# Two moves and seventeen fillers in an attention and experts kernel: output additions ahead of group selection, a third row on VectorE, transposes of the identity in three waits

## The chip, the cores and the metric

The kernel runs on one core of a Trainium2 chip. The metric is the device time of one execution in microseconds, lowest is best. The core has five engines with queues of their own: TensorE (PE, matrix products into the eight banks of PSUM), VectorE (DVE), ScalarE (ACT), GpSimd (POOL) and SyncE (SP, which issues the loads and stores). Each executes its own list of instructions in order; semaphores are the only order between them. An instruction that has to wait holds up everything behind it on its engine.

## The reference

One layer of a transformer, in float32, for 2 sequences of 512 tokens of width 512. The input is normalised, and attention and a mixture of experts both read the normalised tokens; their outputs are added to the input.

```python
xn = _layernorm(x, axis=-1)
x = x + _L0_attn_ref(xn, Wq, Wk, Wv, Wo) + _L0_ffn_ref(xn, router_w, ...)
```

Attention has 32 query heads and 8 key heads of width 128, rotary positions and a causal mask. The feed-forward part has a router over 16 experts in 4 groups, and a shared expert that all tokens pass:

```python
logits = xt @ router_w + router_b
scores = softmax(logits) + router_bias
g = scores.reshape(T, GROUPS, E // GROUPS)
_, gidx = top_k(g.max(axis=-1), LIM)          # the two best groups
masked = where(keep[:, :, None], g, -inf).reshape(T, E)
_, idx = top_k(masked, K)                     # the two best experts in them
...
z = silu(xt @ sw1 + sb1) * (xt @ sw2 + sb2) @ sw3 + sb3   # the shared expert
return (y + z).reshape(shape)
```

## The kernel before

Float32 products are made of three: each operand is split into a rounded high part (`_hi`) and the rest (`_lo`), and `product` issues lo times hi, hi times lo and hi times hi (L1990, L1991, L1992). The high parts are copies on ACT or POOL, the low parts subtractions on DVE or POOL.

The 1024 tokens are eight blocks of 128, four for each sequence (batch 0 and 1). All five lists are written out by hand, in the order in which they run; there is no scheduler. The program has three stages.

First, the normalisation. For each batch DVE takes the statistics of four blocks (`moments`, L1224; `variances`; `scales`), then the blocks are normalised into `xn`: two of them on DVE (L1247), two on ACT (`normalise_rows`, L809). PE transposes the four blocks of a batch into four banks, 16 transposes (`transpose_rows`, L2009); ACT copies each bank to `xT_hi` (`hi_x`, L816), DVE subtracts to `xT_lo` (`lo_x`, L1253). Before `hi_x(0)` ACT also makes the high parts of the first weights of the shared expert (`hi_shared`, L804), from which POOL makes the low parts (L554). Ahead of the first transposes PE runs 38 transposes of the identity (L2086, `WARM`).

Second, the shared expert and the router. PE runs `up_first`, `up(1)`, the router's products, `up(2)`, `up(3)`, then `down(0)` and `down(1)`. `down` makes the output product of one block after the other, six matmuls of 512 columns each, in four banks that are used twice: the product of block n waits until the addition of block n - 4 is done. The wait in the code is `wait_count(pe, down_added, n - 3)`. DVE adds a product to the output `y` (`add_down`, L1310), for which POOL must have added the output's bias to the block before (`add_bias`, L569, counted by `y_biased`). Between, DVE computes the router: softmax, the best groups (`top_groups`, L1340 to L1346), the two best experts (`first_largest`, L1330 to L1356). The low part of the last hidden block is `h_lo` (L1265), which `down(1)` needs at its start.

Third, attention, head after head, with the experts' tiles between. PE first projects keys, values and queries of batch 0 (L1990 to L1992 with `wkv`, L2129 to L2131 with `wq`), while DVE turns the queries by their position (`turn_q1`, `turn_q2`, L1422 to L1430). `first_head(0)` is written out for the first key head: `scores` (L2176), `ranks` (the places of the tokens in the experts' tiles, L2103 to L2109), `project_kv`, and so on. A loop over six key heads and a last head follow.

Of the kernel before, what the change touches and what calls it, by code (L numbers as in the profile page):

```python
# [15 lines left out]
P = 128  # L16
B, T, D = 2, 512, 512
TB = T // P
# [17 lines left out]
S_BANKS, MOE_BANK, PROJ_BANK, OUT_BANKS, PT_BANKS, OT_BANK = (0, 1), 2, 3, (4, 3), (5, 6), 7  # L36
# [14 lines left out]
def wait_count(eng, sem, value):  # L51

    if not isinstance(value, int) or value > 0:
        eng.wait_ge(sem, value)


def count(per_step, g, b, k):

    return (2 * per_step) * g + (per_step * b + k)
# [38 lines left out]
def no_head(g):  # L98

    return isinstance(g, int) and not 0 <= g < KV  # L100
# [7 lines left out]
def build(nc, x, wq, wkv, wo, shared, sb3, w12, w3, b12, b3, router_w, router_b, router_bias,  # L108
# [8 lines left out]
    with ExitStack() as ctx:  # L117
        def sb(name, shape, dt=F32, stack=ctx):
            return stack.enter_context(nc.sbuf_tensor(name, shape, dt))

        def sem(name):
            return ctx.enter_context(nc.semaphore(name))
# [5 lines left out]
        ident = sb("ident", [P, P])  # L128
# [7 lines left out]
        bank = [ctx.enter_context(nc.psum_tensor(f"bank{i}", [P, 512], F32)) for i in range(8)]  # L136
# [107 lines left out]
        scale_ready, xn_dve, xn_act = sem("scale_ready"), sem("xn_dve"), sem("xn_act")  # L244
# [36 lines left out]

        block = ctx.enter_context(nc.Block())

        @block.sync
        def _(sp):

# [238 lines left out]
        def _(pool):  # L525
# [35 lines left out]
            pool.wait_ge(out_bias_in, 16)  # L561

            def add_bias(n):
                b, k = n // TB, n % TB
                if k < 2:
                    pool.wait_ge(xn_dve, 2 * b + k + 1)
                else:
                    pool.wait_ge(xn_act, 2 * b + k - 1)
                nc.gpsimd.tensor_tensor(y[:, n, :], y[:, n, :], out_bias[:, :], ALU.add).then_inc(y_biased, 1)  # L569

            pool.wait_ge(xn_dve, 4)
            for n in range(NB):
                add_bias(n)
            for s in range(2):
# [220 lines left out]
        def _(act):  # L795
# [9 lines left out]

            def normalise_rows(b):
                act.wait_ge(scale_ready, b + 1)
                for n in (TB * b + 2, TB * b + 3):
                    nc.scalar.activation(xn[:, n, :], y[:, n, :], ACT.Identity, bias=lnt[:, 5, n:n + 1],  # L809
                                         scale=lnt[:, 2, n:n + 1]).then_inc(xn_act, 1)  # L810

# [399 lines left out]
        def _(dve):  # L1211
            done = [0]

            def link(ins):

                done[0] += 1
                ins.then_inc(chain, 1)
                dve.wait_ge(chain, done[0])
# [15 lines left out]
            def scales(b):  # L1234
                cols = slice(TB * b, TB * b + TB)
                var, std, inv, tmp, half, shift = (lnt[:, k, cols] for k in range(6))
                dve.wait_ge(std_ready, b + 1)
                link(nc.vector.reciprocal(inv, std))

                nc.vector.tensor_scalar(half, inv, -0.5, None, ALU.mult)  # L1240
                link(nc.vector.tensor_tensor(tmp, inv, inv, ALU.mult))
                link(nc.vector.tensor_tensor(tmp, tmp, var, ALU.mult))
                link(nc.vector.scalar_tensor_tensor(inv, tmp, -3.0, half, ALU.add, ALU.mult))
                nc.vector.scalar_tensor_tensor(shift, mv[:, cols, 0], -1.0, inv, ALU.mult, ALU.mult)\
                    .then_inc(scale_ready, 1)
                for n in (TB * b, TB * b + 1):
                    nc.vector.tensor_scalar(xn[:, n, :], y[:, n, :], mv[:, n, 0:1], lnt[:, 2, n:n + 1],  # L1247
                                            ALU.subtract, ALU.mult).then_inc(xn_dve, 1)

# [57 lines left out]
            def add_down(n):  # L1307
                dve.wait_ge(down_psum, n + 1)
                dve.wait_ge(y_biased, n + 1)
                nc.vector.tensor_tensor(y[:, n, :], y[:, n, :], bank[DOWN_BANKS[n % 4]][:, :], ALU.add)\  # L1310
                    .then_inc(down_added, 1)
# [22 lines left out]
                link(nc.vector.tensor_tensor(result, spare, over_experts(most), ALU.is_equal))  # L1334

            hidden(3)
            for n in range(2):
                add_down(n)
            in_groups = score.rearrange("p n (g e) -> p n g e", g=GROUPS)
            link(nc.vector.tensor_reduce(grp[:, 0], in_groups, AX_X, ALU.max))  # L1340
# [4 lines left out]
                                         grp[:, 1].unsqueeze(3).broadcast_to([P, NB, GROUPS, EG]), ALU.mult))  # L1345
            link(nc.vector.tensor_tensor(masked_groups, masked_groups,  # L1346
                                         grp[:, 2].unsqueeze(3).broadcast_to([P, NB, GROUPS, EG]), ALU.add))
            for n in range(2, TB):
                add_down(n)
            spare, one, two = (pick[:, k] for k in range(3))  # L1350
            first_largest(one, masked, spare)
            link(nc.vector.scalar_tensor_tensor(masked, one, -BIG, masked, ALU.mult, ALU.add))
# [633 lines left out]
        def _(pe):  # L1986
# [10 lines left out]

            def transpose_rows(b):
                for k in range(TB):
                    if k == 0:  # L2000
                        pe.wait_ge(xn_dve, 2 * b + 1)
                    elif k == 1:
                        pe.wait_ge(xn_dve, 2 * b + 2)
                    else:
                        pe.wait_ge(xn_act, 2 * b + (k - 1))
                    for c in range(HC):
                        if k == 0:
                            wait_count(pe, xT_ok, HC * b + c - 3)
                        last = nc.tensor.transpose(bank[TR_BANKS[c]][:, k * P:(k + 1) * P],  # L2009
                                                   xn[:, TB * b + k, c * P:(c + 1) * P], ident[:, :])  # L2010
                        if k == TB - 1:
                            last.then_inc(xT_psum, 1)
# [122 lines left out]
            def project_kv(g, b, i, k, at=None):  # L2135

                if no_head(g):
                    return
                if b == 0 and k == 0:
                    pe.wait_ge(w_split, 6 * g + KV_ORDER)  # L2140
                if at is None and k == 0:
                    pe.wait_ge(q_turned, count(4, g, b, i))
                n = TB * b + 2 * i + k
                cols = slice(n * P, (n + 1) * P)
                last = product(bank[PROJ_BANK if at is None else at][:, k * 2 * P:(k + 1) * 2 * P],
                               [(xT_hi[:, c, cols], xT_lo[:, c, cols],
                                 wkv_hi[:, c].rearrange("p k o -> p (k o)"),
                                 wkv_lo[:, c].rearrange("p k o -> p (k o)")) for c in range(HC)])
                if k == 1:
                    last.then_inc(kv_psum, 1)  # L2150
# [120 lines left out]
            def expert_down(k):  # L2271
# [4 lines left out]
                pe.wait_ge(hT_split, k + 1)  # L2276
                product(bank[MOE_BANK][:, :], [(hT_hi[:, :], hT_lo[:, :], w3_hi[:, :], w3_lo[:, :])]).then_inc(edown_psum, 1)

            def first_ranks(g):

                if isinstance(g, int) and g == 0:
                    ranks()

            def first_head(g):
                scores(g, 0, 0, 0)
                first_ranks(g)
                project_kv(g, 1, 0, 0)
                scores(g, 0, 0, 1)
                project_kv(g, 1, 0, 1)
                scores(g, 0, 1, 0)  # L2290
                scores(g, 0, 1, 1)
                project_q(g, 1, 0, 0)
                project_q(g, 1, 0, 1)
# [505 lines left out]
```

## Time and profile before

| | |
|---|---|
| median of 3 runs | 905.96 us (905.58 to 906.03) |
| the profiled execution in all | 905.59 us |
| its span in the trace | 903.8 us |
| PE, DVE, ACT, POOL busy | 888.5, 677.7, 431.2, 526.5 us |
| granted TensorE clock, mean | 1.00 |

Times in the trace count from the start of the span. Busy is the time in which at least one instruction of an engine was at work; matmuls overlap, so PE's consecutive starts and not their durations tell its pace.

### The profile page before, as it was taken

To read this page: it belongs to the slowest core of one execution; us is meant where nothing else is said; L and a number is where in the kernel's file an instruction comes from. 1 tells how busy PE (TensorE), PEld (TensorE's weight loads), DVE (VectorE), ACT (ScalarE), POOL (GpSimd) and SP (SyncE) were. 2 spreads that over 40 slices of the span, in tenths; PEclk is the share of its full clock that TensorE was granted. 3 is DMA by queue.
4 is the path that set the end of the run, shared out by engine and by line. 5 is a ranking of instruction groups with operands and counts; after the bars stand their busy time and mean duration, and the time that the engine had idled before them with its cause. 6 is when DMAs were issued, how large, how long until landed. Compare 5 with 4: busy or idle time off the path is not lost.

```text
span 903.8 us, 17478 instructions
## 1 busy us (share of the span) xinstructions
PE 888.5 (98%) x5066; PEld 762.2 (84%) x5066; DVE 677.7 (75%) x1614; ACT 431.2 (48%) x1083; POOL 526.5 (58%) x638
## 2 busy tenths in 40 slices
PE   8997999999999999999999999999999999999998
PEld 7786887888888888888888889888888888888886
DVE  6688876687767876768767786768776787676886
ACT  3504543554535644454554545445453564454543
POOL 5923786565654765538554575356565476543663
PEclk9999999999999999999999999999999999999999
DMA  9910223143223532335222443224322252230242
GB/s 329 319 47 15 92 94 123 42 131 121 88 76 86 172 95 79 90 99 168 87 87 76 114 163 87 75 81 126 123 87 75 89 172 94 80 92 22 84 150 94
DMA packets 52161, 97.73 MB, mean 108 GB/s; under 512 B 5920, under 2 KB 17824, under 8 KB 52128
## 3 DMA queue, kind: packets, MB, share of 16 engines
q1 hardware_dynamic: 49568, 88.94, 31.7%
q0 software_dynamic: 2560, 8.39, 2.8%
q8 instruction: 16, 0.26, 0.1%
q14 instruction: 17, 0.14, 0.1%
HBM read 74.76 MB, written 22.54 MB: 108 GB/s over the span
## 4 chain that ended last, share of the span: by engine, by line
PE 92%; DVE 5%; issue 1%; ACT 1%; DMA 0%; POOL 0%; SPq 0%; DVEq 0%
PE bank L1992 10%; PE bank L1990 10%; PE bank L1991 10%; PE bank L2190 7%; PE bank L2129 7%; PE bank L2131 6%; PE bank L2130 6%; PE bank L2226 6%; PE bank L2222 6%; PE bank L2223 6%; PE bank L2206 4%; PE bank L2203 4%; PE bank L2204 4%; PE bank L2251 1%; PE bank L2176 1%
## 5 line engine op out<-in xcount | busy, mean ns | idle before, releaser
L636 POOL TENSOR_SCALAR prob<-prob,rsum 128x128 f32<-128x128 f32 (+3 forms) x256 | 143.9, 582 | 89.8 <-DVE rsum L1480 89.1
L876 ACT ACTIVATE prob<-bank,nmax 128x128 f32<-128x128 f32 (+3 forms) x256 | 133.7, 528 | 113.9 <-DVE nmax L1474 111.3
L1474 DVE CUSTOM_DVE_ANT_0 bank<-bank,causal 128x128 f32<-128x128 f32 (+3 forms) x256 | 122.8, 501 | 35.5 <-PE bank L1992 33.7
L1502 DVE TENSOR_TENSOR pT_lo<-bank,pT_hi 128x512 fp32r<-128x512 f32 x160 | 109.1, 684 | 29.0 <-ACT pT_hi L896 28.6
L896 ACT ACTIVATE pT_hi<-bank 128x512 fp32r<-128x512 f32 x160 | 95.0, 596 | 67.1 <-PE bank L2190 53.4
L2222 PE MATMUL bank<-wo_lo,oT_hi 128*128 128x512 f32 x256 | 106.2, 415 | 0.0
L2129 PE MATMUL bank<-xT_hi,wq_lo 128*128 128x512 f32 x256 | 104.7, 409 | 1.5 <-DVE v_lo L1458 1.4
L619 POOL TENSOR_TENSOR w_lo<-w_raw,w_hi 128x1024 fp32r<-128x1024 f32 x31 | 74.3, 2398 | 52.7 <-ACT w_hi L931 52.7
L2131 PE MATMUL bank<-xT_hi,wq_hi 128*128 128x512 f32 x256 | 101.1, 395 | 0.0
L2226 PE MATMUL bank<-wo_hi,oT_lo 128*128 128x512 f32 x256 | 100.7, 393 | 0.0
L2130 PE MATMUL bank<-xT_lo,wq_hi 128*128 128x512 f32 x256 | 100.6, 393 | 0.0
L2223 PE MATMUL bank<-wo_hi,oT_hi 128*128 128x512 f32 x256 | 100.5, 392 | 0.0
L585 POOL TENSOR_TENSOR q_first<-rot 128x128 f32<-128x128 f32 x60 | 28.3, 472 | 115.3 <-DVE rot L1430 115.1
L2190 PE MATMUL bank<-ident,prob 128*128 128x128 f32 x640 | 94.1, 272 | 0.0
L2190 PEld LDWEIGHTS bank<-ident,prob 128*128 128x128 f32 x640 | 77.7, 140 | 13.5
L1990 PE MATMUL bank<-wkv_hi,xT_lo 128*128 128x256 f32 x256 | 74.7, 292 | 1.1 <-DVE prob L1430 0.8
L1992 PE MATMUL bank<-wkv_hi,xT_hi 128*128 128x256 f32 x256 | 72.3, 282 | 0.0
L1991 PE MATMUL bank<-wkv_lo,xT_hi 128*128 128x256 f32 x256 | 71.9, 281 | 0.0
L1990 PE MATMUL bank<-kT_hi,q_lo 128*128 128x256 f32 (+2 forms) x192 | 68.0, 354 | 3.1 <-ACT prob L876 2.9
L887 ACT ACTIVATE oT_hi<-bank 128x512 fp32r<-128x512 f32 x64 | 38.1, 595 | 65.9 <-PE bank L2206 65.2
L2203 PE MATMUL bank<-pT_hi,v_lo 128*128 128x512 f32 x160 | 65.5, 409 | 0.5 <-DVE oT_lo L1487 0.5
L1991 PE MATMUL bank<-kT_lo,q_hi 128*128 128x256 f32 (+2 forms) x192 | 64.7, 337 | 0.0
(219 smaller groups left out, 2326.5 us busy)
## 6 DMA issues: line engine op xcount, KB each, us to landing
w_raw<-w SPq DMA_DIRECT2D x31, 512.0 KB, 3.5
wq_raw<-wq SPq DMA_DIRECT2D x32, 256.0 KB, 4.1
wo_raw<-wo SPq DMA_DIRECT2D x32, 256.0 KB, 2.8
xg<-x_slots SPq DMA_DIRECT2D x31, 256.0 KB, 3.5
w_raw<-w SPq DMA_DIRECT2D x31, 256.0 KB, 2.8
eb<-b SPq DMA_DIRECT2D x31, 256.0 KB, 3.9
y_slots<-eb SPq DMA_DIRECT2D x31, 256.0 KB, 2.5
x_slots<-pairs SPq DMA_DIRECT2D x3, 2048.0 KB, 16.0
```

Of the source, the lines that this page charges most:

```text
L636: last = nc.gpsimd.tensor_scalar(row, row, rsum[:, stat(b, i, h)], 1.0, ALU.mult, ALU.mult)
L876: last = nc.scalar.activation(prob[n % 2][:, h, 0:P * (i + 1)], bank[S_BANKS[use % 2]][:, 256 * k:256 * k + P * (i + 1)], ACT.Exp, bias=nm ...
L1990: nc.tensor.matmul(dst, a_lo, c_hi, start=start and k == 0, stop=False)
L1991: nc.tensor.matmul(dst, a_hi, c_lo, start=False, stop=False)
L1992: last = nc.tensor.matmul(dst, a_hi, c_hi, start=False, stop=stop and k == len(terms) - 1)
L2129: nc.tensor.matmul(q, wq_lo[:, h, col], xT_hi[:, c, span], start=c == 0, stop=False)
L2130: nc.tensor.matmul(q, wq_hi[:, h, col], xT_lo[:, c, span], start=False, stop=False)
L2131: last = nc.tensor.matmul(q, wq_hi[:, h, col], xT_hi[:, c, span], start=False, stop=c == HC - 1)
L2190: last = nc.tensor.transpose(bank[PT_BANKS[n % 2]][:, h * P:(h + 1) * P], prob[nth(g, b, i) % 2][:, h, j * P:(j + 1) * P], ident[:, :])
L2222: nc.tensor.matmul(dst, oT_hi[:, k, h], wo_lo[:, h, :], start=h == 0, stop=False)
L2223: nc.tensor.matmul(dst, oT_hi[:, k, h], wo_hi[:, h, :], start=False, stop=False)
L2226: last = nc.tensor.matmul(dst, oT_lo[:, k, h], wo_hi[:, h, :], start=False, stop=h == G - 1)
```

## The change

Three parts. The first changes which engine normalises which block: in batch 0 DVE takes blocks 0, 1 and 2 and ACT block 3; batch 1 stays at two and two. PE and POOL wait for the blocks accordingly. The second moves the additions of blocks 2 and 3 on DVE ahead of the group selection. The third puts transposes of the identity, which read and give nothing that is used, at three places of the first key head on PE: six after `ranks`, four and seven around `scores(g, 0, 1, 0)`; they write bank 7, which is free there.

```diff
+        DVE_ROWS, ACT_ROWS = (0, 1, 2, 4, 5), (3, 6, 7)
+
+        def wait_row(engine, n):
+            if n in DVE_ROWS:
+                engine.wait_ge(xn_dve, DVE_ROWS.index(n) + 1)
+            else:
+                engine.wait_ge(xn_act, ACT_ROWS.index(n) + 1)
...
-            pool.wait_ge(xn_dve, 4)
+            pool.wait_ge(xn_dve, len(DVE_ROWS))
...
-                for n in (TB * b + 2, TB * b + 3):
+                for n in ACT_ROWS[b:2 * b + 1]:
...
-                for n in (TB * b, TB * b + 1):
+                for n in DVE_ROWS[3 * b:3 * b + 3]:
...
             hidden(3)
-            for n in range(2):
+            for n in range(TB):
                 add_down(n)
             in_groups = score.rearrange("p n (g e) -> p n g e", g=GROUPS)
...
-            for n in range(2, TB):
-                add_down(n)
             spare, one, two = (pick[:, k] for k in range(3))
...
+            def keep_busy(g, k):
+
+                if isinstance(g, int) and g == 0:
+                    for _ in range(k):
+                        nc.tensor.transpose(bank[OT_BANK][:, 0:P], ident[:, :], ident[:, :])
...
             def first_head(g):
                 scores(g, 0, 0, 0)
                 first_ranks(g)
+                keep_busy(g, 6)
                 project_kv(g, 1, 0, 0)
                 scores(g, 0, 0, 1)
                 project_kv(g, 1, 0, 1)
+                keep_busy(g, 4)
                 scores(g, 0, 1, 0)
+                keep_busy(g, 7)
                 scores(g, 0, 1, 1)
```

The lists of the built programs show it in place. On ACT, at the start, the list before reads (a row is the line, the operation, what it writes and reads, and what it waits for; `xn` is a normalised block, `ew_hi` a weight's high part):

```order
L800 ACTIVATE lnt<-lnt 128x4 [waits var_ready]
L809 ACTIVATE xn<-y,lnt 128x512 [waits scale_ready]
L809 ACTIVATE xn<-y,lnt 128x512
L804 ACTIVATE ew_hi<-eraw 128x512 [waits eraw_first_in0]
L804 ACTIVATE ew_hi<-eraw 128x512 [waits eraw_first_in1]
L816 ACTIVATE xT_hi<-bank 128x512 [waits xT_psum] x4
```

and that of the change:

```order
L804 ACTIVATE lnt<-lnt 128x4 [waits var_ready]
L813 ACTIVATE xn<-y,lnt 128x512 [waits scale_ready]
L808 ACTIVATE ew_hi<-eraw 128x512 [waits eraw_first_in0]
L808 ACTIVATE ew_hi<-eraw 128x512 [waits eraw_first_in1]
L820 ACTIVATE xT_hi<-bank 128x512 [waits xT_psum] x4
```

One block less stands ahead of the weights and of the transposed input; on DVE a third one stands ahead of the statistics of batch 1. On DVE, behind the last hidden block, the list before reads (`y<-y,bank` is an output addition, `grp` and `beat` belong to the group selection, `red` and `pick` to the two best experts):

```order
L1265 TENSOR_TENSOR h_lo<-hid,h_hi 128x512 [waits h_hi_ok,h_ok]
L1310 TENSOR_TENSOR y<-y,bank 128x512 [waits y_biased,down_psum] x2
L1340 TENSOR_REDUCE grp<-route 128x32
L1319 TENSOR_TENSOR beat<-grp 128x128 [waits chain]
L1320 TENSOR_TENSOR beat<-grp 128x128 [waits chain]
L1321 TENSOR_TENSOR beat<-beat,before 128x128 [waits chain]
L1323 TENSOR_TENSOR beat<-beat 128x128 [waits chain]
L1324 TENSOR_REDUCE grp<-beat 128x32 [waits chain]
L1325 TENSOR_SCALAR grp<-grp 128x32 [waits chain]
...
L1346 TENSOR_TENSOR route<-route,grp 128x128 [waits chain]
L1310 TENSOR_TENSOR y<-y,bank 128x512 [waits y_biased,down_psum,chain]
L1310 TENSOR_TENSOR y<-y,bank 128x512 [waits y_biased,down_psum]
```

and that of the change:

```order
L1269 TENSOR_TENSOR h_lo<-hid,h_hi 128x512 [waits h_hi_ok,h_ok]
L1314 TENSOR_TENSOR y<-y,bank 128x512 [waits y_biased,down_psum] x4
L1344 TENSOR_REDUCE grp<-route 128x32
L1323 TENSOR_TENSOR beat<-grp 128x128 [waits chain]
L1324 TENSOR_TENSOR beat<-grp 128x128 [waits chain]
...
L1350 TENSOR_TENSOR route<-route,grp 128x128 [waits chain]
L1334 TENSOR_REDUCE red<-route 128x8 [waits chain]
```

The third and fourth addition went from behind the ten steps of the group selection to ahead of them. On PE, in the first key head, the list of the change has (the `ident` rows are the new ones; everything else stands as before):

```order
L2106 MATMUL bank<-chosen,ones 128x16 x8
L2280 MATMUL bank<-ident 128x128 x6
L1992 MATMUL bank<-wkv_hi,xT_lo 128x256 [waits q_turned]
...
L1994 MATMUL bank<-wkv_hi,xT_hi 128x256
L2280 MATMUL bank<-ident 128x128 x4
L1992 MATMUL bank<-kT_hi,q_lo 128x256 [waits exps_ok,q_split]
...
L1994 MATMUL bank<-kT_hi,q_hi 128x256
L2280 MATMUL bank<-ident 128x128 x7
L1992 MATMUL bank<-kT_hi,q_lo 128x256 [waits exps_ok,q_split]
```

Each group of fillers stands directly ahead of an instruction that waits, and waits for nothing itself.

## Rows read from the trace of the kernel before

**Rows 1.** The page: the span, and busy time of PE.
```profile
span 903.8 us, 17478 instructions
...
PE 888.5 (98%) x5066; PEld 762.2 (84%) x5066; DVE 677.7 (75%) x1614; ACT 431.2 (48%) x1083; POOL 526.5 (58%) x638
```

**Rows 2.** Waits of PE, whole span: us in total, times, longest.
```profile
PE bank L1990 <- DVE y L1310: 1.0, 1, 1.0
...
PE bank L2041 <- ACT xT_hi L816: 0.6, 1, 0.6
```

**Rows 3.** Timeline of ACT, 0 to 40: start us, us, line, operation [idle before].
```profile
9.02 1.52 ACT L809 ACTIVATE xn<-y,lnt 128x512 f32<-128x512 f32 x2 [1.11 <-DVE lnt L1244]
10.44 1.14 ACT L804 ACTIVATE ew_hi<-eraw 128x512 fp32r<-128x512 f32 x2
11.49 2.03 ACT L816 ACTIVATE xT_hi<-bank 128x512 fp32r<-128x512 f32 x4
...
22.11 2.07 ACT L816 ACTIVATE xT_hi<-bank 128x512 fp32r<-128x512 f32 x4 [2.59 <-PE bank L2009]
```

**Rows 4.** Timeline of PE, 0 to 60, its start-up.
```profile
2.57 6.62 PE L2086 MATMUL bank<-ident 128*128 128x128 f32 x38 [2.57 <-POOL ident L533]
9.49 1.99 PE L2009 MATMUL bank<-ident,xn 128*128 128x128 f32 x16 [0.30 <-DVE xn L1247]
12.11 2.19 PE L2041 MATMUL bank<-xT_hi,ew_hi 128*128 128x512 f32 x8 [0.63 <-ACT xT_hi L816]
...
15.96 1.98 PE L2051 MATMUL bank<-xT_lo,ew_hi 128*128 128x512 f32 x8
...
20.49 1.91 PE L2009 MATMUL bank<-ident,xn 128*128 128x128 f32 x16
```

**Rows 5.** Timeline of DVE, 0 to 40.
```profile
8.90 1.00 DVE L1247 TENSOR_SCALAR xn<-y,mv,lnt 128x512 f32<-128x512 f32 x2
9.81 2.47 DVE L1224 BATCH_NORM_STATS2 stats<-y 128x6 f32<-128x512 f32 x4
...
12.73 1.03 DVE L1232 TENSOR_SCALAR lnt<-mv 128x4 f32<-128x4 f32 x1
```

**Rows 6.** Timeline of POOL, 0 to 60.
```profile
11.22 2.52 POOL L554 TENSOR_TENSOR ew_lo<-eraw,ew_hi 128x512 fp32r<-128x512 f32 x2 [7.49 <-ACT ew_hi L804]
```

**Rows 7.** Timeline of DVE, 40 to 105.
```profile
44.26 0.83 DVE L1265 TENSOR_TENSOR h_lo<-hid,h_hi 128x512 fp32r<-128x512 f32 x1 [0.77 <-ACT h_hi L827]
45.01 1.27 DVE L1310 TENSOR_TENSOR y<-y,bank 128x512 f32<-128x512 f32 x2
...
49.22 1.28 DVE L1310 TENSOR_TENSOR y<-y,bank 128x512 f32<-128x512 f32 x2
...
61.60 0.69 DVE L1422 TENSOR_TENSOR rot<-bank,qc 128x512 f32<-128x512 f32 x1 [1.09 <-PE bank L2131]
...
64.39 0.69 DVE L1422 TENSOR_TENSOR prob<-bank,qc 128x512 f32<-128x512 f32 x1 [0.70 <-PE bank L2131]
```

**Rows 8.** Timeline of PE, 0 to 60, the output products of batch 1.
```profile
46.02 0.39 PE L1990 MATMUL bank<-ew_hi,h_lo 128*128 128x512 f32 x1
...
48.57 0.40 PE L1992 MATMUL bank<-ew_hi,h_hi 128*128 128x512 f32 x1
49.96 0.50 PE L1990 MATMUL bank<-ew_hi,h_lo 128*128 128x512 f32 x1 [0.98 <-DVE y L1310]
```

**Rows 9.** Timeline of PE, 60 to 100, waits around the fillers' places.
```profile
72.96 0.39 PE L1990 MATMUL bank<-wkv_hi,xT_lo 128*128 128x256 f32 x1 [0.82 <-DVE prob L1430]
...
77.60 0.36 PE L1990 MATMUL bank<-kT_hi,q_lo 128*128 128x256 f32 x1 [0.62 <-ACT prob L876]
...
79.59 0.35 PE L1990 MATMUL bank<-kT_hi,q_lo 128*128 128x256 f32 x1 [1.04 <-ACT prob L876]
...
80.82 0.50 PE L2129 MATMUL bank<-xT_hi,wq_lo 128*128 128x512 f32 x1 [0.29 <-DVE v_lo L1458]
```

**Rows 10.** Windows: busy us and instructions by engine, granted clock (PEclk), DMA share, GB/s.
```profile
70.00:90.00 20.00, 15.44 (x109) 12.75 (x108) 16.96 (x56) 8.73 (x26) 7.62 (x12) 1.00 0.05 15
```

More of the change, by code:

```diff
@@ L563, in add_bias @@
             def add_bias(n):
[L564 to L568, printed above, removed]
+                wait_row(pool, n)
                 nc.gpsimd.tensor_tensor(y[:, n, :], y[:, n, :], out_bias[:, :], ALU.add).then_inc(y_biased, 1)
-            pool.wait_ge(xn_dve, 4)
+            pool.wait_ge(xn_dve, len(DVE_ROWS))
             for n in range(NB):
@@ L1999, in transpose_rows @@
                 for k in range(TB):
[L2000 to L2005, printed above, removed]
+                    wait_row(pe, TB * b + k)
                     for c in range(HC):
```

## The prediction, written before the changed kernel ran

> **What bounds the kernel now.** The page comes first: TensorE (PE) is busy for 888.5 of the span's 903.8 us [rows 1], so only what lets PE start its work earlier can shorten the run, and at most some 15 us are there to be had. The list of waits, for PE, says which: the two that this change can touch are 1.0 us, once, for the output addition on VectorE (DVE), and 0.6 us, once, for the rounded copy of the transposed input on ScalarE (ACT) [rows 2]. The timelines then place them: the ACT wait ends at 12.11 us, the DVE wait at 49.96 us [rows 4, 8]. The three places of the fillers are PE waits of 0.82, 0.62 and 1.04 us, ending at 72.96, 77.60 and 79.59 us [rows 9]. Last the stretch from 70 to 90 us as a whole: PE busy 15.44 of 20 us, granted clock 1.00, the 2.4 GHz level [rows 10]. Between 12 us and 48.8 us PE has no wait of its own, so an earlier start there is handed on whole; what hands it on after that is checked below.
>
> **Part one, the normalised rows.** Before, ACT does two rows of batch 0 and then two rounded copies of the first weights, and only then the first copy of the transposed input, at 11.49 us; it stands in a row without a gap: rows from 9.02, weights from 10.44, transposed input from 11.49 [rows 3]. A row costs ACT (10.44 - 9.02) / 2 = 0.71 us of its time. With one row less the weights run from 9.73 to about 10.87 (their 1.14 us), and ACT is free 0.6 us sooner than now. Then PE's transposes decide. They need row 2 from DVE: DVE's pitch is (9.81 - 8.90) / 2 = 0.46 us and the second row ends at 9.90, so the third ends at about 10.35 [rows 5]. PE's 16 transposes start 0.115 us apart ((1.99 - 0.27 for the last one) / 15) from 9.49, so those of row 2 start at about 10.41 [rows 4]: DVE is ready 0.06 us ahead. They keep their times. When could ACT begin then? Batch 1 shows it with a free ACT: transposes from 20.49, first copy at 22.11, so 1.62 us later [rows 3, 4]; add the 0.08 us by which batch 0's block is longer (1.99 against 1.91) and it is 9.49 + 1.70 = 11.19 us. That is 11.49 - 11.19 = 0.30 us sooner. PE's first real matmul follows the first copy after 0.62 us and after it the copies set the pace (four in 2.03 us), so the whole block moves: **-0.30 us**. Its bounds: 0.15 if the DVE row is late by as much as its own margin twice over and semaphores take the rest; 0.60 if PE's last transposes did not matter and ACT's freedom were all that counts.
>
> What this makes later: DVE's statistics of batch 1 start 0.46 us later, at 10.27. At 12.73 a tiny DVE operation took 1.03 us, up to 13.76; GpSimd's (POOL) two splits run until 13.74 [rows 5, 6]. DVE waited there for POOL, so most of the 0.46 us is swallowed, since POOL's splits now also start up to 0.7 us sooner. The low part that DVE then makes is needed by PE only from 15.96 us, two microseconds on. Cost 0.
>
> The Trainium skill (SBUF — State Buffer, "SBUF: two separate sides") says that one port pair is shared by VectorE and GpSimd as an exclusive lock, and whichever begins first blocks the other for its whole instruction. This trace agrees, by the 1.03 us at 12.73. The rule speaks against a third SBUF-to-SBUF row on DVE: if POOL's split got in first, the row would be held for a split's 1.26 us and part one would lose about 0.6 us rather than gain. The third row starts at 9.81, and POOL can't begin before ACT's first weight copy ends at about 10.35, so I give that little.
>
> **Part two, the output additions.** PE's last output product but one (token block 6 of 8) reuses the bank of block 2 and waits until three additions are done. The products of block 5 end with the one that starts at 48.57; the next would start one step (0.23) later, at 48.80. It starts at 49.96 and takes 0.50 us where the one before took 0.40 [rows 8]. So the wait costs 49.96 - 48.80 + 0.10 = 1.26 us. In DVE's order two additions run from 45.01 to 46.28, group selection follows, and the third addition starts only at 49.22 [rows 7]. Moved up, the third runs from 46.28 to 46.9 and the fourth to 47.5 (0.60 us each). Are their products there? A block is six matmuls of 0.23 us, 1.40 us, and block 4's begin at 46.02 [rows 8]; so block 3's are out at about 46.2 and block 2's 1.4 us earlier, against additions that start at 46.9 and 46.3. Both are. PE wants the third at 48.80 (48.50 with part one) and has it 1.6 us before. **-1.26 us**; the low bound is 1.0, the idle time alone. Group selection starts 1.2 us later, but the steps behind it (the two largest) start where they did, since the same additions stood in front of them: DVE's total is the same, and the expert choice isn't delayed.
>
> Next to be late is h_lo, DVE at 44.26 for 0.83 us [rows 7], which PE's block 4 product wants at 46.02 [rows 8]. It has 0.9 us, or 0.6 when PE comes 0.30 sooner and DVE doesn't.
>
> Does the gain get through to 70 us? DVE turns the query projections into rotated ones and waits for PE there: 1.09 us before 61.60, 0.70 us before 64.39 [rows 7]. PE brings both 1.56 us sooner. If DVE doesn't move at all it starts the first 1.05 us sooner, ends it 0.5 us late against PE, and the 0.70 us make that up: it is busy with it for 64.39 - 0.70 - 61.60 = 2.09 us, so until 60.51 + 0.04 + 2.09 = 62.64, against 64.39 - 1.56 = 62.83. From there the whole chain of DVE, POOL and ACT to 81 us hangs on PE and moves as one. Behind 110 us PE hardly waits, so nothing absorbs it.
>
> **Part three, the fillers.** Nothing in the trace has exactly their place. The nearest rows are the transposes of rows 4: 0.115 us a piece in a warm stream, 6.62 / 38 = 0.174 us for the same instruction in the kernel's first microseconds [rows 4]. Six, four and seven cost 0.69, 0.46 and 0.81 us by the first and 1.04, 0.70 and 1.22 by the second; the waits are 0.82, 0.62 and 1.04 [rows 9]. By the first value all seventeen lie inside waits. I take it, because PE comes to the fillers out of 60 us of nearly unbroken work, as the transposes at 9.49 come out of a stream, and not from rest as the first 38 do. By the second they overrun by 0.22, 0.08 and 0.18, 0.48 us together, and even that has cover: PE still waits 0.29 us for DVE at 80.82 [rows 9], and the work that DVE, POOL and ACT do meanwhile doesn't come from the delayed products at once. **0**, with bounds of -0.3 (three restarts, each 0.1 us quicker because PE isn't idle in front) and +0.5.
>
> The waits' length doesn't change by parts one and two, since their two ends move together. The granted clock is 1.00 in this stretch already, so there is no clock to win back [rows 10]. The Trainium skill (TensorE: Matmul & The Clock Gate, "HAM oscillation — how this bites in real kernels") says that long idle gaps of the array let its clock fall to half and advises against them; by it fillers would pay where that happens. In this trace it doesn't happen, so by row and rule the sum is the same; only if other executions did fall would the page give more.
>
> **The sum.** -0.30 - 1.26 + 0 = -1.56 us. The profiled execution took 905.59 us in all, so its like would take 904.03; the median of the three runs is 0.37 us above it, 905.96, and from there 904.40. I forecast 904.4 us, 0.17% less. A measurement of this kernel tells about 0.2%, 1.8 us, from no change, so the likeliest result lies just inside that.
>
> **The rivals.**
> The gain arrives as summed (chance 0.58): with the bounds 0.15 to 0.6, 1.0 to 1.26 and 0.3 us between executions, 903.8 to 905.0.
>
> More than that (0.18): the restarts come quicker (0.3 us), or DVE's locks fall more kindly and ACT is freed by the full 0.6: up to 2.2 us, 903.4 to 903.9. For it speaks that each restart begins with a longer matmul, 0.50 against 0.40 for a 512-column one [rows 8]; against it that those products aren't what the chain waits for. A mild form is that the clock did fall in unprofiled runs: they differ by only 0.45 us, so it could give no more than that, 904.0.
>
> Less (0.18): DVE comes later than now. Its small steps from 38 to 44 us work on SBUF alone while POOL splits weights without a break, as the one at 12.73 did [rows 5, 6], and POOL's and DVE's phases now shift against each other; one more split to wait for is 1.3 us. Then h_lo misses its 0.6 us of cover and PE waits 0.7 us at block 4: 905.1. Or only part two works: 904.7. That the additions moved don't shorten anything would need block 3's product to come late, over 1 us later than it does.
>
> Slower than before (0.06): the fillers aren't covered. If they stand in front of products that were ready, all seventeen at 0.174 us are 2.96 us, less 1.56 gained: 907.4. It turns to slower once more than 1.56 us of them lie bare, that is more than half. Against it: three measured waits of 2.48 us in sum.
>
> **How the numbers follow.** The range leaves out the top of the last rival and the far ends: 903.6 to 905.6, which holds the first case, most of the less case and half of the second. Faster by over 0.2% means below 904.15: the whole of the second case, 0.18, and a third of the first, 0.18 more, 0.36 together. Slower by over 0.2% is above 907.8, which only a bad form of the last case reaches, 0.03. The rest, 0.61, is within 0.2%.
>
> **What the profile afterwards would show.** Part one: ACT's first copy of the transposed input near 11.2 us and the first matmul behind it near 11.8. Part two: no PE wait for the addition, the block 6 products starting one 0.23 us step behind block 5's, the key and value projections near 51.3 instead of 52.86. Part three: fillers of six, four and seven ending before their waits do, each wait's end 1.56 us earlier than now, and remaining idle times of 0.1 to 0.3 us. I am wrong if a new wait stands at 45 to 46 us for h_lo, if DVE's first rotation doesn't start by 60.6, or if the products behind the fillers start less than 1.4 us earlier than before.

## The result and the profile after

| | before | with the change |
|---|---|---|
| median, same chip | 906.38 us (20 runs) | 904.89 us (20 runs, 903.99 to 905.8) |
| ratio, 95% interval | | 0.9982 [0.9976, 0.9988] |
| the profiled execution in all | 905.59 us | 905.0 us |
| its span | 903.8 us | 903.2 us |
| granted TensorE clock, mean | 1.000 | 0.999 |

The change saves 0.18%, 1.6 us by the ratio: real by its interval, and just inside the 0.2% that the prediction called "no change". 904.4 us was forecast; 904.89 us was measured. Of the 0.49 us between them 0.42 is the starting point: the forecast started from 905.96 us, the median of three runs, and the twenty runs of the kernel before beside the change have 906.38. Three single runs of 1254, 1785 and 5045 us (two of the kernel before, one of e8) are left out of the ratios, means and counts below.

The page of the changed kernel, beside [rows 1]:

```profile
span 903.2 us, 17512 instructions
...
PE 890.6 (99%) x5083; PEld 764.3 (85%) x5083; DVE 676.9 (75%) x1615; ACT 430.2 (48%) x1082; POOL 525.8 (58%) x638
```

PE has the seventeen fillers more, DVE a normalised block more and ACT one less. The timeline of ACT at the start, beside [rows 3]:

```profile
9.08 0.81 ACT L813 ACTIVATE xn<-y,lnt 128x512 f32<-128x512 f32 x1 [1.11 <-DVE lnt L1248]
9.80 1.14 ACT L808 ACTIVATE ew_hi<-eraw 128x512 fp32r<-128x512 f32 x2
11.28 2.07 ACT L820 ACTIVATE xT_hi<-bank 128x512 fp32r<-128x512 f32 x4 [0.34 <-PE bank L2006]
```

The row of transposed copies now has an idle time of 0.34 us, and its releaser is PE: ACT is free before the first bank is ready, and PE's transposes decide. The timeline of DVE, beside [rows 5, 7]:

```profile
8.96 1.46 DVE L1251 TENSOR_SCALAR xn<-y,mv,lnt 128x512 f32<-128x512 f32 x3
10.33 2.47 DVE L1228 BATCH_NORM_STATS2 stats<-y 128x6 f32<-128x512 f32 x4
...
13.25 0.47 DVE L1236 TENSOR_SCALAR lnt<-mv 128x4 f32<-128x4 f32 x1
...
43.60 0.81 DVE L1269 TENSOR_TENSOR h_lo<-hid,h_hi 128x512 fp32r<-128x512 f32 x1 [0.77 <-ACT h_hi L831]
44.34 2.47 DVE L1314 TENSOR_TENSOR y<-y,bank 128x512 f32<-128x512 f32 x4
```

Three blocks in 1.46 us; the tiny operation that took 1.03 us takes 0.47; four additions stand together. The timeline of PE, beside [rows 4, 8, 9]:

```profile
9.56 2.01 PE L2006 MATMUL bank<-ident,xn 128*128 128x128 f32 x16
11.93 2.21 PE L2038 MATMUL bank<-xT_hi,ew_hi 128*128 128x512 f32 x8 [0.36 <-ACT xT_hi L820]
...
48.41 0.40 PE L1994 MATMUL bank<-ew_hi,h_hi 128*128 128x512 f32 x1
48.66 0.40 PE L1992 MATMUL bank<-ew_hi,h_lo 128*128 128x512 f32 x1
...
51.44 0.28 PE L1992 MATMUL bank<-wkv_hi,xT_lo 128*128 128x256 f32 x1
...
70.51 0.86 PE L2280 MATMUL bank<-ident 128*128 128x128 f32 x6
71.47 0.39 PE L1992 MATMUL bank<-wkv_hi,xT_lo 128*128 128x256 f32 x1
...
75.32 0.60 PE L2280 MATMUL bank<-ident 128*128 128x128 f32 x4
76.11 0.35 PE L1992 MATMUL bank<-kT_hi,q_lo 128*128 128x256 f32 x1 [0.19 <-ACT prob L880]
...
76.89 0.93 PE L2280 MATMUL bank<-ident 128*128 128x128 f32 x7
78.10 0.36 PE L1992 MATMUL bank<-kT_hi,q_lo 128*128 128x256 f32 x1 [0.28 <-ACT prob L880]
```

Block 6's products follow block 5's after 0.25 us, with no idle time. The ends of the three waits stood at 72.96, 77.60 and 79.59 [rows 9] and stand at 71.47, 76.11 and 78.10: 1.49 us earlier each. So at 80 us 1.49 us are won, and yet the two profiled spans differ by 0.6 only. Matmul by matmul PE is still 1.57 us ahead at 210.74 and 0.63 us at 217.79: the rest was given back there, in rows that the change doesn't touch. SP's queue, ACT and PE of the changed kernel, 199 to 218 us:

```profile
199.62 0.33 SPq L364 DMA_DIRECT2D w_raw<-w  x1
206.86 1.07 ACT L935 ACTIVATE w_hi<-w_raw 128x1024 fp32r<-128x1024 f32 x1 [2.32 <-DMA w_raw<-w]
217.79 0.39 PE L1992 MATMUL bank<-wkv_hi,xT_lo 128*128 128x256 f32 x1 [0.78 <-DVE rot L1432]
```

An expert's 512 KB of weights were issued at 199.62 and landed just before 206.86. The same two in the kernel before, where PE has no wait behind them:

```profile
201.49 0.33 SPq L356 DMA_DIRECT2D w_raw<-w  x1
207.00 1.06 ACT L931 ACTIVATE w_hi<-w_raw 128x1024 fp32r<-128x1024 f32 x1 [0.81 <-DMA w_raw<-w]
```

There the load took 5.5 us (207.00 - 201.49), here 7.2. Whether that is cause or chance is what the last experiment is for.

### The profile page after: what moved, and what is told of

Read it like the earlier page. It is cut to its first block, busy times and chain, and to the rows that moved or that the text cites. A ratio compares the mean times of both kernels' runs of the same rounds, so it can differ in the third digit from the quotient of the medians.

```text
span 903.2 us, 17512 instructions
## 1 busy us (share of the span) xinstructions
PE 890.6 (99%) x5083; PEld 764.3 (85%) x5083; DVE 676.9 (75%) x1615; ACT 430.2 (48%) x1082; POOL 525.8 (58%) x638
## 4 chain that ended last, share of the span: by engine, by line
PE 90%; DVE 4%; issue 3%; POOL 2%; ACT 1%; DMA 0%; another core or an unknown queue 0%; SPq 0%; DVEq 0%; POOLq 0%
PE bank L1992 10%; PE bank L1994 10%; PE bank L1993 10%; PE bank L2187 7%; PE bank L2126 6%; PE bank L2128 6%; PE bank L2127 6%; PE bank L2219 6%; PE bank L2223 6%; PE bank L2220 6%; PE bank L2203 4%; PE bank L2200 4%; PE bank L2201 4%; PE bank L2173 1%; PE bank L2248 1%
## 5 line engine op out<-in xcount | busy, mean ns | idle before, releaser
L1994 PE MATMUL bank<-kT_hi,q_hi 128*128 128x256 f32 (+2 forms) x192 | 64.7, 337 | 0.0
```

Source lines behind the costliest of these rows:

```text
L1994: last = nc.tensor.matmul(dst, a_hi, c_hi, start=False, stop=stop and k == len(terms) - 1)
```

## The experiments

Time is given as the ratio to runs of the kernel before on the same chip, whose median was 904.34 us in the first group of four kernels, 904.47 in the second and 904.54 in the third. As these ratios carry about 0.9 us of uncertainty, small terms are read from the traces, between two fixed points of one execution. Three are used: DVE's first normalised block (D), PE's first real matmul (M), PE's first key projection (K).

| kernel | D | M | M - D | K | K - D |
|---|---|---|---|---|---|
| before | 8.90 | 12.11 | 3.21 | 52.86 | 43.96 |
| before again | 8.72 | 11.94 | 3.22 | 52.67 | 43.95 |
| the change | 8.96 | 11.93 | 2.97 | 51.44 | 42.48 |
| rows alone | 8.75 | 11.71 | 2.96 | 52.02 | 43.27 |
| additions alone | 9.13 | 12.34 | 3.21 | 51.83 | 42.70 |
| fillers alone | 8.31 | 12.00 | 3.69 | 52.23 | 43.92 |
| no fillers | 8.85 | 11.81 | 2.96 | 51.33 | 42.48 |
| the change again | 8.73 | 11.68 | 2.95 | 51.20 | 42.47 |
| four blocks on DVE | 8.97 | 12.91 | 3.94 | 52.47 | 43.50 |

D itself varies between executions, from 8.31 to 9.29 us, since it hangs on the first loads. Between kernels with the same start M - D repeats within 0.02 us and K - D within 0.05, with one exception in M - D. In the profile of the fillers alone the loads came early, and PE was then still at its 38 transposes of the identity, which lasted until 9.90: its transposes of `xn` start at 9.73, and M - D is 3.69.

**e1_rows: the first part alone.** Additions and fillers as before. (In e1 to e3 the blocks are given by the same two lists as in the change; the first line below is the division of the kernel before.)

```diff
-        DVE_ROWS, ACT_ROWS = (0, 1, 4, 5), (2, 3, 6, 7)
+        DVE_ROWS, ACT_ROWS = (0, 1, 2, 4, 5), (3, 6, 7)
```

> The third row on VectorE alone. My theory: PE's wait for the output addition is still there and ends with VectorE's chain, so what counts at 50 us is how much earlier VectorE is, not how much earlier PE is. In the profile of the full change VectorE's additions began at 44.34 instead of 45.01, 0.67 us sooner, because GpSimd's splits had moved up too. So at 90 us this kernel should stand 0.6 to 0.7 us ahead of before, 0.07% of the time. The rival, that the parts simply add up as my prediction summed them, says 0.2 to 0.3 us.

Measured: 903.51 us, 0.9987 [0.9978, 0.9996]. K - D falls by 0.69 us: 0.25 of it up to the first matmul, 0.44 behind. The wait for the addition shows where the 0.44 come from; in the kernel before it was 0.98 us [rows 8]. Timeline of PE:

```profile
49.11 0.50 PE L1994 MATMUL bank<-ew_hi,h_lo 128*128 128x512 f32 x1 [0.48 <-DVE y L1314]
```

DVE comes to its first addition at 44.15, 35.40 us behind D, where it was 36.11 before: 0.71 us less. POOL sets this, as DVE's `h_lo` of the block before shows. Timelines of DVE and POOL in the kernel before:

```profile
36.67 1.42 DVE L1265 TENSOR_TENSOR h_lo<-hid,h_hi 128x512 fp32r<-128x512 f32 x1 [0.77 <-ACT h_hi L827]
36.25 1.29 POOL L547 TENSOR_TENSOR wkv_lo<-wkv_raw,wkv_hi 128x512 fp32r<-128x512 f32 x1
```

and in e1:

```profile
36.32 0.92 DVE L1269 TENSOR_TENSOR h_lo<-hid,h_hi 128x512 fp32r<-128x512 f32 x1 [0.77 <-ACT h_hi L831]
35.40 1.29 POOL L555 TENSOR_TENSOR wkv_lo<-wkv_raw,wkv_hi 128x512 fp32r<-128x512 f32 x1
```

In both DVE's operation ends 0.55 us after POOL's split. Relative to D, 0.20 of the 0.71 us is there before this operation starts and 0.50 comes off its length. POOL's list moved as a whole, because ACT gives it the first high part sooner: its first split starts 1.61 us behind D instead of 2.32. In the four profiles in which PE waits for the addition, K stands 41.64 us (before), 41.63 (before again), 41.66 (e1) and 41.61 (e3) behind the start of that split. So the first part shortens this wait by itself, by way of POOL.

**e2_adds: the second part alone.**

```diff
             hidden(3)
-            for n in range(2):
+            for n in range(TB):
                 add_down(n)
...
-            for n in range(2, TB):
-                add_down(n)
```

> The output additions moved up alone. My theory: PE goes straight through the output products and gains 1.26 us there; the first transposed copy stays where it was. At 90 us 1.2 to 1.3 us ahead of before, ratio about 0.9986. The rival that additions moved don't help without the third row (VectorE's h_lo too late for block 4) says under 1.0 us and a new wait near 46 us.

Measured: 902.7 us, 0.9984 [0.9974, 0.9993]. K - D falls by 1.26 us, M - D doesn't move, and the wait for `y` is gone. In this profiled execution the granted clock fell. Timeline of PE, a wait just ahead of it, and windows (busy us and instructions by engine, clock, DMA share, GB/s):

```profile
71.85 0.39 PE L1992 MATMUL bank<-wkv_hi,xT_lo 128*128 128x256 f32 x1 [0.81 <-DVE prob L1432]
```

```profile
72.00:73.00 1.00, 1.00 (x8) 1.00 (x9) 0.38 (x1) 0.00 (x0) 1.00 (x2) 0.76 0.00 0
73.00:75.00 2.00, 2.00 (x11) 2.00 (x11) 0.75 (x4) 1.29 (x2) 0.66 (x1) 0.50 0.00 0
```

For some 3.4 us PE ran at 0.50, the 1.2 GHz level. It cost nothing here: the slower products ended within the wait before the scores (0.62 us in the kernel before), and from K to attention's first output product, the first matmul with `wo`, it is 44.45 us as in the changed kernel.

**e3_fill: the third part alone.**

```diff
                 first_ranks(g)
+                keep_busy(g, 6)
                 project_kv(g, 1, 0, 0)
```

(and the groups of four and seven, as in the change).

> The seventeen fillers alone. My theory: they lie in waits; at 90 us PE stands within 0.05 us of before, the median within 0.05%. The rival, that the fillers carry part of the gain by holding the clock in executions that are not profiled, says a median 0.3 us or more lower and no runs above 907 us, where the kernel before had 5 of 20 above it.

Measured: 903.98 us, 0.9997 [0.9988, 1.0006]. K to the first output product takes 44.55 us, 44.54 without fillers. They cost nothing and bring nothing that the time alone can show. The rival's other sign, runs above 907 us, says nothing here: among the runs on this chip the kernel before has none either.

**e4_nofill: rows and additions, no fillers.**

```diff
-                keep_busy(g, 6)
...
-                keep_busy(g, 4)
...
-                keep_busy(g, 7)
```

> Rows and additions without the fillers. My theory: the whole gain, 1.50 us ahead of before at 90 us and a ratio of about 0.9983, the same as the full change within 0.03%. The rival (fillers hold the clock) says a ratio nearer 0.9990 and single runs 2 to 3 us above the fastest.

Measured: 902.14 us, 0.9977 [0.9967, 0.9988], the same as with them (e5, on another chip, 0.9976). K - D is that of the whole change. But this profiled execution, too, had a fall of the clock, at another place. PE's timeline ahead of it, and windows:

```profile
77.99 0.37 PE L1992 MATMUL bank<-kT_hi,q_lo 128*128 128x256 f32 x1 [1.04 <-ACT prob L880]
```

```profile
78.00:79.00 1.00, 1.00 (x5) 1.00 (x6) 0.86 (x4) 0.64 (x2) 0.60 (x1) 0.60 0.00 0
79.00:81.00 2.00, 2.00 (x7) 1.62 (x6) 1.90 (x10) 1.02 (x4) 0.81 (x2) 0.50 0.00 0
81.00:82.00 1.00, 1.00 (x4) 0.76 (x3) 0.96 (x6) 0.00 (x0) 0.76 (x3) 0.69 0.00 0
```

and the stretch behind it, K to the first output product, took 45.52 us, where without a fall it is 44.43 to 44.58 in the eleven other profiles (e7 apart). Here, with no wait close behind that takes it up, a fall costs 1.0 us.

**e5_full and e6_control: the whole change and the kernel before, once more.** No edit.

> The whole change once more, beside the experiments of this call. My theory: at 90 us about 1.5 us ahead of the kernel before, ratio 0.9982 to 0.9984, and no execution whose mean granted clock is 0.998. The rival, that the first measurement's 0.18% was in part luck of late stalls after 130 us, says a ratio of 0.9990 or above.

> The kernel before, unchanged, with a profile of its own. Ratio 1.0000 within 0.06% by every theory; it gives the trace for comparison at 90 us. In a third of the executions of before the mean granted clock was 0.998; if this profile is one, the dip should stand between 70 and 85 us, where PE's waits are dense, and move the start of the products at 90 us by 0 to 1.0 us.

Measured: the change 902.36 us, 0.9976 [0.9966, 0.9986]; the kernel before 904.77 us, 1.0003 [0.9994, 1.0012]. The comparison of two like kernels doesn't favour a side. The change gains more here than in the first measurement (2.1 us against 1.5 between medians), but the two intervals overlap from 0.9976 to 0.9986, where the forecast 0.9982 to 0.9984 lies too. No run of the change has a mean clock of 0.998.

**e7_fill3x: three times the fillers.**

```diff
-                keep_busy(g, 6)
+                keep_busy(g, 18)
...
-                keep_busy(g, 4)
+                keep_busy(g, 12)
...
-                keep_busy(g, 7)
+                keep_busy(g, 21)
```

> Three times the fillers (18, 12 and 21) with rows and additions as in the change. A filler takes 0.11 to 0.12 us in the profile of the change, so the added 34 are 3.9 us, and the idle time left at these places was 0.1, 0.19 and 0.28 us. My theory: what goes beyond the waits comes onto PE's path almost whole, 2.0 to 3.3 us against the change, ratio to before 1.0005 to 1.002. The rival, that the chain of VectorE and ScalarE hides it because the products behind the fillers aren't what it waits for, says under 1 us against the change.

Measured: 903.44 us, 0.999 [0.9982, 0.9999], 1.1 us above e5. Timeline of PE:

```profile
70.39 2.16 PE L2280 MATMUL bank<-ident 128*128 128x128 f32 x18
...
75.70 1.47 PE L2280 MATMUL bank<-ident 128*128 128x128 f32 x12
...
77.73 2.45 PE L2280 MATMUL bank<-ident 128*128 128x128 f32 x21
```

A filler takes 0.11 us ((2.16 - 0.27) / 17), the pace of the transposes at 9.49. Against e5, aligned at K, PE is 0.96 us late behind the first group, 1.96 at most and 1.41 from 86 us on: what goes beyond the waits is paid, but waits further on take a part back. My theory had said 2.0 to 3.3 us on the path, a ratio above 1.0005, and the rival under 1 us; it lies between, so the theory priced the overrun too high.

**e8_rows4: the fourth block on DVE as well.**

```diff
-        DVE_ROWS, ACT_ROWS = (0, 1, 2, 4, 5), (3, 6, 7)
+        DVE_ROWS, ACT_ROWS = (0, 1, 2, 3, 4, 5), (6, 7)
```

> All four rows of batch 0 on VectorE, the rest as in the change. My theory: with three rows PE's transposes and no longer ScalarE decide when the transposed input can be copied, so freeing ScalarE further gives nothing: the first matmul stands 2.9 to 3.0 us behind VectorE's first row as in the change (3.21 before), the time is the change's within 0.05%. The rival, that ScalarE is still the bound (the 0.60 us end of my range), says 0.3 us less; a late fourth row says up to 0.3 us more.

Measured: 902.77 us, 0.9975 [0.9966, 0.9984]; by the time alone not to be told from the change. By the trace it is 1.0 us worse at M - D. Timelines of DVE, POOL and PE:

```profile
8.97 2.87 DVE L1251 TENSOR_SCALAR xn<-y,mv,lnt 128x512 f32<-128x512 f32 x4
10.05 2.92 POOL L562 TENSOR_TENSOR ew_lo<-eraw,ew_hi 128x512 fp32r<-128x512 f32 x2 [6.32 <-DVE xn L1251]
11.89 0.66 PE L2006 MATMUL bank<-ident,xn 128*128 128x128 f32 x4 [0.75 <-DVE xn L1251]
12.91 2.19 PE L2038 MATMUL bank<-xT_hi,ew_hi 128*128 128x512 f32 x8 [0.36 <-ACT xT_hi L820]
```

Four blocks take 2.87 us instead of some 1.9 (three take 1.46, at a pitch of 0.46): with no block to make, ACT gives POOL its weights at once, and POOL starts its first split at 10.05, while DVE's third block (9.88 to 10.42) is running and ahead of the fourth, at 10.34. The first split takes 1.50 us instead of 1.28, and the fourth block 1.50 instead of 0.54: it ends 0.29 us after the split. The Trainium skill (SBUF — State Buffer, "SBUF: two separate sides") says that of a VectorE operation in a 2-port mode or with two SBUF inputs and a GpSimd operation, the one that starts first gets the shared port pair for its whole instruction and the other is blocked; this trace agrees, by that 1.0 us. Three blocks is where the margin ends.

**e10_six, e11_fourseven, e12_none: which fillers keep the clock.** The change with the first group only; with the second and third only; and without any (the kernel of e4 again).

```diff
-                keep_busy(g, 4)
...
-                keep_busy(g, 7)
```

> Rows and additions as in the change, and only the first group of fillers, the six behind the ranks. Part three was found to cost nothing, but executions without any fillers had a mean granted clock of 0.998 in about a quarter of their runs, and those with all seventeen in none of 53. If the first place protects the clock (the fall seen at 72 us in the run with the additions alone began there), no run has 0.998. If the third place does (the fall seen at 78 us in the run without fillers began there), about a quarter of the runs still have it, 2 to 3 of ten. Time in either case within 0.3 us of the whole change: the six are hidden in a wait of 0.82 us.

```diff
-                keep_busy(g, 6)
```

> Rows and additions as in the change, and only the second and third group of fillers, four and seven. The other half of the question of the run before: if the first place decides, about a quarter of the runs have a mean clock of 0.998; if the second and third do, none. If each wait can start a fall by itself, both this one and the one before have some. Time within 0.3 us of the whole change.

> Rows and additions without any filler, a second time, on the chip on which the two halves of the fillers run: the rate of runs with a mean clock of 0.998 to set the others against, 2 to 4 of ten expected (3 of 8 the first time). Its median is expected within 0.3 us of the one with six fillers and the one with eleven; if the fillers were worth what a fall of the clock costs each time (1.0 us) in each execution, it would lie 0.3 us above them in the mean.

Measured: 902.96 us, 0.9981 [0.9971, 0.999]; 902.56 us, 0.9975 [0.9966, 0.9983]; 902.57 us, 0.9979 [0.9969, 0.9989]. Each run's record has its mean granted clock, and one of 0.998 or less marks a fall (3.4 us at half speed are 1.7 of 900 us; where in the run it stood, only a profile shows). Over all runs that have such a record:

| fillers | runs | with a fall |
|---|---|---|
| none (before, control, e1, e2, e4, e12) | 136 | 41 |
| six only (e10) | 12 | 5 |
| four and seven only (e11) | 12 | 3 |
| both, or more (the change, e3, e5, e7, e8, e9) | 66 | 0 |

So the rate is 30% without fillers, neither half removes it, and all three groups together do. Twenty of the 66 runs were on the first chip, where the kernel before has no clocks on record; on the three chips with both it is 41 of 136 against 0 of 46. e12 by itself has 1 of 9, where 2 to 4 of ten were expected, and one run of the kernel before has a far lower mean, 0.948. As both halves have some, a fall can start at more than one place. The price: in e10 the runs with a fall take 904.02 us in the mean and the others 902.21; in e11 902.29 and 902.52; in the kernel before, over its 87 runs in three groups, the runs with a fall are 0.2, 0.4 and 0.5 us longer. At 30% of the runs that is 0.1 us in the mean, less than any ratio here resolves.

**e9_w12first: the late weights.** The whole change, and in the loop over the key heads the load of the second tile's first weights goes ahead of two bias loads on SP.

```diff
                 e2 = load_x(tile_of(g, 2))
+                load_w12(tile_of(g, 2), e2)
                 load_b3(tile_of(g, 1), e1)
                 load_b12(tile_of(g, 2), e2)
-                load_w12(tile_of(g, 2), e2)
```

> The whole change, and in the loop over the key heads the load of the second tile's first weights (512 KB) issued ahead of two small bias loads instead of behind them. My theory: the stall of 0.78 us at 217.79 in the profiled execution of the changed kernel, where the rotation on VectorE came late, begins with this load, which was issued at 199.62 and landed only at 206.9, where ScalarE had waited for it for 2.32 us. The last product that reads the old weights has ended by 194.5, so the load can be issued some 3.2 us sooner, near 196 instead of 199.6. Then ScalarE's rounded copy of these weights no longer waits for the transfer (idle before it under 0.3 us, against 0.56 to 2.32 us), no execution has the late rotation at 217.79, and the mean over runs falls by 0.2 to 0.6 us against the whole change. The rival: the load was not what was late (PE and VectorE only phase against each other there); then the time is the same within 0.2 us and the stall is still seen in some executions. A second rival: a transfer issued sooner collides with the stores and loads of that moment and delays another, and the time is longer by up to 0.5 us.

Measured: 901.5 us (five runs, 901.15 to 901.77), 0.9964 [0.9952, 0.9977]. SP's queue and ACT in this kernel:

```profile
195.56 0.34 SPq L364 DMA_DIRECT2D w_raw<-w  x1
202.53 1.06 ACT L935 ACTIVATE w_hi<-w_raw 128x1024 fp32r<-128x1024 f32 x1
```

and ACT and PE in e5, at the same place of a later head:

```profile
633.74 1.06 ACT L935 ACTIVATE w_hi<-w_raw 128x1024 fp32r<-128x1024 f32 x1 [2.56 <-DMA w_raw<-w]
644.67 0.39 PE L1992 MATMUL bank<-wkv_hi,xT_lo 128*128 128x256 f32 x1 [0.78 <-DVE rot L1432]
```

Counted from K, the load is issued 2.8 us earlier than in e5 (195.56 - 51.78 against 197.81 - 51.20); ACT waits for it in neither head, and neither stall is there. The fourteen profiles of this study have 28 such places, near 205 and 634 us. In the twelve where ACT's idle time before `w_hi` is 1.60 us or more, PE waits for the rotation some eleven microseconds on; in the sixteen where it is 1.45 or less it never does:

| ACT's idle before `w_hi` | 0 to 1.45 | 1.60 | 1.72 | 1.82 | 1.84 | 1.85 | 2.11 | 2.18 | 2.32 to 2.56 (5) |
|---|---|---|---|---|---|---|---|---|---|
| PE's wait behind it | none | 0.16 | 0.25 | 0.35 | 0.38 | 0.41 | 0.65 | 0.73 | 0.78 to 0.80 |

The traces show that the late load makes the stall. The time points the same way (mean 901.46 us beside 902.46 to 902.97 for e10, e11 and e12, on the same chip), but more strongly than forecast (0.2 to 0.6 us): the stalls at the two places come to 0.6 us in the mean of the eleven profiles that have some part of the change and the old order of loads, and where the rest of the 1.0 us or more comes from isn't shown. It is five runs, the whole change without the edit wasn't run on that chip, and the interval overlaps that of e5. Nor is it shown that the change has no part in the stalls: e3, with fillers alone, has one, but the kernel before has none at its four places, and its loads wait up to 1.45 us, just short.

## Why the prediction was right

**What bounds.** PE's timeline, and there the waits of [rows 2]: right. What came off the two waits arrived at 80 us whole.

**Part one, -0.30 us.** ACT's first copy was expected near 11.2 and stands at 11.28; the first matmul near 11.8, and stands at 11.93. Relative to DVE's first block the gain is 3.21 - 2.97 = 0.24 us; DVE's own start, 8.96 against 8.90, took 0.06 of it back in this execution. The reasoning by the free ACT held: copy behind transposes by 1.72 us, 1.70 expected. Taken together with part two it is right, alone it is too small: e1 shows 0.69. The text said that POOL's splits would start up to 0.7 us sooner and that a late DVE would be swallowed, and booked nothing for it. It stopped too early: the operation at 12.73 does take 0.47 us instead of 1.03, but that alone is lost again, as DVE idles for 2.5 us before 35.15 in any case. What lasts is POOL's lead of 0.71 us, which DVE meets again from 36 us on, and with which it stands 0.7 us better at its first addition. Where PE waited for just that addition, the first part has a gain that the second also has. That the forecast didn't suffer is because the second part removes this wait.

**Part two, -1.26 us.** Exactly the 1.26 us of e2. In the whole change the two give 1.48 to 1.49, not 0.69 + 1.26 = 1.95, because a wait that is gone can't be shortened by an earlier DVE; the sum of -0.30 and -1.26 was right as it stood, since the 0.30 had been worked out for a PE without that wait.

**Part three, 0.** Right for the path: e3, and e4 beside e5. All three groups end within their waits; by pieces they take 0.11 to 0.12 us, the first of the two prices weighed. The remaining idle times, 0.10 (70.51 + 0.86 to 71.47), 0.19 and 0.28 us, lie in the forecast 0.1 to 0.3.

**The clock.** The step "in this trace it doesn't happen" was true of the trace and not of the kernel. A fall to half stands in 30% of the runs without fillers and in none with all of them. The Trainium skill (TensorE: Matmul & The Clock Gate, "HAM oscillation — how this bites in real kernels") speaks of long idle gaps; the ones just ahead of the two falls in the traces are 0.81 and 1.04 us, among several others, and which of PE's idle times count no run here separates. The prediction had kept this as a mild form of its "more" case, with up to 0.45 us; the measured mean is near 0.1 us, too little to show in the sum.

**The rivals.** "More" by quicker restarts: not seen, K to the first output product is the same with fillers as without. "Less" by a late `h_lo`: PE's block 4 starts on time, at 45.87, and DVE was earlier, not later: the shift between POOL and DVE that this rival feared took place and went the other way (e1). "Slower" by bare fillers: needs three times as many, and even e7's are faster than the kernel before.

**Getting through.** -1.49 us at 80 us and -1.6 by the ratio (-2.1 in e5) agree with "behind 110 us nothing absorbs it" in the mean. A single pair of profiles would have said -0.6, because one of them had the late weights and the other had not.

## What to carry to other kernels

When two edits feed the same wait, work out each with the other in place: alone they were worth 0.69 and 1.26 us, together 1.49. Compare traces between two points of the same execution, which repeated here within 0.02 to 0.05 us (but for one execution in which another engine set the start, e3), and not by their spans, where a late transfer hundreds of microseconds away adds or hides as much as the whole change. And look through every run's clock, not only the profiled one's: filler work in a wait cost nothing here as long as it was shorter than the wait, and what it prevents may show in one run of three only.

The version to keep is e9: the change with the weight load ahead, 901.5 us, 0.36% under the kernel before by five runs.

## What was not expected of the hardware

The granted clock can fall to 0.50 for some 3.4 us in the middle of a kernel whose PE is busy 98% of the time, behind idle times of only 0.81 and 1.04 us (e2, e4). The mean clock shows such a fall in 41 of 136 runs and not in the others of the same programs. Fillers in one or two of the three waits left it (8 of 24 runs), fillers in all three removed it (0 of 66). Why a given run falls stays open, and so does whether fewer than seventeen fillers would do in all three places.

The 512 KB load took 5.5 us from issue to landing in one execution, 7.2 in another, at the same place of a nearly identical program. ACT could be idle for up to 1.45 us there without a wait of PE (1.60 us gave 0.16), and the difference decided between no wait and 0.8 us of PE.
